# Attention scores: one copy of 1097 columns out of PSUM in place of two copies with a maximum each

## What is computed

```
attn = q @ k.T * SCALE                       # 1097 x 1097, head dimension 8
kth  = the 137th largest score of each row   # top_k = 1097 // 8
attn = softmax(where(attn >= kth, attn, -inf))
out  = attn @ v
```

## Time and profile before

| | |
|---|---|
| median of 3 runs | 11960.32 us (11940.51 to 11967.36) |
| the profiled execution | 11958.84 us, of which the span is 11957.0 us |
| busy over the span | DVE 9191.7 us (77%), PE 8171.2 us (68%), ACT 6947.3 us (58%), POOL 2151.1 us (18%) |
| the attention stage | 3009 to 10121 us from the span's start, 128 steps |
| copies out of PSUM (L1281) | 1280 from `a_psS`, 889.7 us busy; 1024 from `a_psT`, 703.0 us |

### The profile page before, as it was taken

One profiled execution on the slowest core, in us unless ns is written; L12 is line 12 of the kernel. 1 busy time (PEld: TensorE's weight loads), 2 busy tenths in 40 slices (PEclk: granted clock), 3 DMA queues, 4 the chain that ended last, 5 costly groups with the idle time before them and its releaser, 6 DMA issues. The chain is left out here.

```text
span 11957.0 us, 167569 instructions
## 1 busy us (share of the span) xinstructions
PE 8171.2 (68%) x45521; PEld 5352.0 (45%) x45521; DVE 9191.7 (77%) x26006; ACT 6947.3 (58%) x11527; POOL 2151.1 (18%) x1960
## 2 busy tenths in 40 slices
PE   5555477777486765667878687876667768343899
PEld 4555455555243433334444344443334434233787
DVE  8999644444898988999999899998889989644333
ACT  0000011221697976878999799997788979122222
POOL 2323211111000000000000000000000000277666
PEclk9999955555566655656666666665666656555555
DMA  3222100000000000000000000000000000243211
GB/s 91 73 68 72 33 19 20 20 19 21 14 16 16 17 12 14 13 16 17 17 17 18 14 15 18 18 18 14 13 14 17 18 12 16 43 96 79 55 54 40
DMA packets 669893, 352.03 MB, mean 29 GB/s; under 512 B 587281, under 2 KB 605680, under 8 KB 665056
## 3 DMA queue, kind: packets, MB, share of 16 engines
q1 hardware_dynamic: 607920, 242.84, 9.5%
q0 software_dynamic: 58624, 60.72, 2.0%
q10 hardware_dynamic: 2384, 37.11, 0.9%
HBM read 200.20 MB, written 147.72 MB: 29 GB/s over the span
## 5 line engine op out<-in xcount | busy, mean ns | idle before, releaser
L1049 PE MATMUL a_psT<-a_qt,a_kt 74*122 74x366 bf16 x3456 | 1554.8, 450 | 969.1 <-ACT a_pT L1130 632.0
L1138 ACT ACTIVATE a_junk<-a_s,a_aim 122x1097 bf16<-122x1097 f32 x1152 | 1378.9, 1208 | 721.3 <-DVE a_s L1281 721.3
L1214 DVE MAX8 a_near<-a_below 122x8 f32<-122x274 f32 (+1 forms) x4608 | 1699.2, 430 | 0.1
L1052 PEld LDWEIGHTS a_psT<-a_weigh,a_drops 122*122 122x122 bf16 x10368 | 1571.0, 190 | 192.0
L1207 DVE SCALAR_TENSOR_TENSOR a_below<-a_s,a_te,a_signs 122x1097 f32<-122x1097 f32 x1152 | 1546.4, 1352 | 129.2 <-remote 128.3
L1130 ACT ACTIVATE a_pT<-a_psT 122x732 f32<-122x732 f32 (+1 forms) x1920 | 1371.6, 715 | 455.4 <-PE a_psT L1052 447.9
L1052 PE MATMUL a_psT<-a_weigh,a_drops 122*122 122x122 bf16 x10368 | 1522.5, 273 | 0.0
L1138 ACT ACTIVATE a_signs<-a_s,a_te 122x1097 bf16<-122x1097 f32 x1152 | 1400.9, 1219 | 4.4 <-DVE a_te L1199 4.4
L1065 PE MATMUL a_psO<-a_pT,a_v 122*32 122x366 f32 x6912 | 1401.3, 698 | 0.0
L1138 ACT ACTIVATE a_junk<-a_s,a_te 122x1097 bf16<-122x1097 f32 x1152 | 1389.2, 1209 | 0.0
L1049 PEld LDWEIGHTS a_psT<-a_qt,a_kt 74*122 74x122 bf16 x3456 | 616.8, 178 | 1667.0 <-issue 1648.1
(11 more groups left out here) (356 smaller groups left out, 14795.9 us busy)
## 6 DMA issues: line engine op xcount, KB each, us to landing
xbuf<-r_blank ACTq DMA_DIRECT2D x16, 1990.6 KB
e_xg<-xbuf SPq DMA_DIRECT2D x56, 568.8 KB, 4.3
r_bc<-pr SPq DMA_DIRECT2D x16, 1372.0 KB, 7.4
a_k<-kT SPq DMA_DIRECT2D x384, 51.5 KB
a_q<-qT SPq DMA_DIRECT2D x384, 51.5 KB
a_kt<-kT SPq DMA_DIRECT2D x384, 51.5 KB
a_qt<-qT SPq DMA_DIRECT2D x384, 51.5 KB
r_xt<-in_x SPq DMA_DIRECT2D x16, 784.0 KB
```

The costliest lines, as they stand in the source:

```text
L1049: pe.matmul(out[:, x, 0:CW], kt[q][:, u * QP:(u + 1) * QP], qt[q][:, c * CW:(c + 1) * CW], start=True, stop=False)
L1052: mm = pe.matmul(out[:, x, t * QP:(t + 1) * QP], drops[:, c * CT + t, u * QP:(u + 1) * QP], weigh[:, :], start=False, stop=t == CT - 1)
L1138: act.activation(out[:, :], s_[:, t, :], ACT.Sign, bias=at[:, t:t + 1], scale=-1.0, accum_out=total[:, t:t + 1]).then_inc(counted[r], 1)
L1214: mx = dve.max(near[:, t, g, :], below[t % 3][:, EDGES[g]:EDGES[g + 1]])
```

## The change

A score tile now lies in consecutive columns for odd tiles too: `psT[0]` and `psT[1]` become two halves of one PSUM tensor `a_psB` of 4 banks, and an odd score tile takes its first 1097 columns. One DVE instruction copies the whole tile and keeps one maximum straight in `a_peak`; the `tensor_tensor` over the two maxima goes, and a bare semaphore increment stands in its place. PE raises `scored` once per tile, on the third matmul, and waits for `evacuated` once per tile, ahead of the first matmul; all counts of these two semaphores are halved accordingly. The fills keep their places in PSUM. No operation, transfer or tile is added.

```diff
-        peaks = sb("a_peaks", [QP, 2, QT])
-        psT = [ps(f"a_psT{i}", [QP, 2, 512]) for i in range(2)]
+        psB = ps("a_psB", [QP, 2048])
+        psT = [psB[:, 1024 * i:1024 * (i + 1)].rearrange("p (x n) -> p x n", x=2) for i in range(2)]
...
         def score_banks(t):
-            if t % 2:
-                return (psT[i][:, :, :].rearrange("p x n -> p (x n)") for i in range(2))
-            return psS[0:QP, 0:HALF], psS[0:QP, HALF:3 * HALF]
+            return (psB if t % 2 else psS)[0:QP, 0:MN]
...
-                wait(pe, evacuated, 2 * n - 1 if t == 0 else 2 * n - 3)
+                wait(pe, evacuated, n if t == 0 else n - 1)
                 apart(pe, k)
                 q_ = qs[o][:, t * QP:(t + 1) * QP]
-                low, high = score_banks(t)
-                pe.matmul(low[:, 0:HALF], q_, ks[o][:, 0:HALF], start=True, stop=True).then_inc(scored, 1)
+                out = score_banks(t)
+                pe.matmul(out[:, 0:HALF], q_, ks[o][:, 0:HALF], start=True, stop=True)
...
-                wait(pe, evacuated, 2 * n if t == 0 else 2 * n - 2)
...
-                pe.matmul(high[:, 0:HALF], q_, ks[o][:, HALF:2 * HALF], start=True, stop=True)
-                pe.matmul(high[:, HALF:MN - HALF], q_, ks[o][:, 2 * HALF:MN], start=True, stop=True).then_inc(scored, 1)
+                pe.matmul(out[:, HALF:2 * HALF], q_, ks[o][:, HALF:2 * HALF], start=True, stop=True)
+                pe.matmul(out[:, 2 * HALF:MN], q_, ks[o][:, 2 * HALF:MN], start=True, stop=True).then_inc(scored, 1)
...
-                banks = tuple(score_banks(t))
-                for i, (a, b) in enumerate(((0, HALF), (HALF, MN))):
-                    wait(dve, scored, 2 * (QT * (s + 1) + t) + i + 1)
-                    dve.tensor_scalar(sc[o][:, t, a:b], banks[i][:, 0:b - a], 1.0, None, ALU.mult, ALU.max,
-                                      accum_out=peaks[:, i, t:t + 1]).then_inc(evacuated, 1)
+                wait(dve, scored, QT * (s + 1) + t + 1)
+                dve.tensor_scalar(sc[o][:, t, :], score_banks(t), 1.0, None, ALU.mult, ALU.max,
+                                  accum_out=peak[:, t:t + 1]).then_inc(evacuated, 1)
...
                 if ahead:
-                    wait(dve, evacuated, 2 * QT * (s + 2))
-                    dve.tensor_tensor(peak[:, :], peaks[:, 0, :], peaks[:, 1, :], ALU.max).then_inc(peaked, 1)
+                    wait(dve, evacuated, QT * (s + 2))
+                    dve.sem_inc(peaked, 1)
```

More of the change, by code:

```diff
@@ L984, in step @@
                 if not isinstance(s, int) or s + 2 < HEADS:
-                    wait(sp, scored, 2 * QT * (s + 1))
+                    wait(sp, scored, QT * (s + 1))
                     operands(s + 2, qs[p], ks[p], s_in[p])
@@ L1079, in turn_back @@
                 wait(pe, o_out, CHUNKS * (s - 2))
-                wait(pe, evacuated, 2 * QT * done(s + 1))
+                wait(pe, evacuated, QT * done(s + 1))
                 wait(pe, flagged, 2 * done(s - 1))
@@ L1091, in step @@
                 if last:
-                    wait(pe, evacuated, 2 * QT * done(s + 1) - 2)
+                    wait(pe, evacuated, QT * done(s + 1) - 1)
                     for i in range(2):
@@ L1173, in step @@
                             wait(act, aimed, 5 * s + 6)
-                        wait(act, evacuated, 2 * (QT * (s + 1) + t + 1))
+                        wait(act, evacuated, QT * (s + 1) + t + 1)
                         if t >= 2:
```

## The result

The changed kernel takes 12015.45 us (median of 8 runs, 11978.02 to 12019.67), the kernel before on the same chip 11939.69 us (8 runs, 11919.42 to 11967.36): a ratio of 1.0053, 95% interval 1.0038 to 1.0068. The ratio is estimated from all runs of both kernels; the quotient of the two medians alone would be 1.0063. The changed kernel is slower, as forecast, and within the range given (11955 to 12030).

What follows compares the result with a forecast made beforehand. DVE's copies were taken to bound the attention stage, and PE's answer after the change. 91 steps gave +44.6 us, 13 gave -1.6, the others 0: 11958.84 + 43 + 1.5 = 12003 us, range 11955 to 12030.

Steps and rivals of the forecast that it cites:

- The body: Back-to-back copies of a step after tile 0's first; claimed paced by DVE before the change, with PE early.
- C: Way round for two tiles: copy with read 1.30, signal 0.15, PE's refill 0.89, signal 0.30; 2.64 us.
- the ordinary step: Step where DVE waited for tile 0; 11.50 us before, 11.99 after, +0.49 in 91 steps.
- The sum of the copies: Change over all 128 attention steps: 44.6 - 1.6 = +43 us.
- late steps: Up to 24 steps, one shown with ACT bounding the end; -0.08 to +0.10 us each, taken as 0.
- The ready steps: 13 steps with tile 0 ready and both its copies counted; 12.11 to 11.99 us, -0.12 each, -1.6 together.
- The last `tensor_tensor`: 0.17 us at each step's end, taken as hidden behind the sequencer: its removal gains 0, otherwise 22 us.
- Edits costed at nothing: ACT's later counts, PE's first fills of the next step and fewer PE register and semaphore instructions; 0 us.
- T0: Moment in each step when tile 0 is complete and its last copy can start; claimed not to move.
- ACT's cover: Time from tile 4 copied out to ACT beginning on it; about 1.9 us, claimed to hide later copies.
- the faster rival: PE answers in time in the body, needing its 2.4 GHz clock; 11915 to 11937 us, chance 0.07.
- the slowest rival: Wide copy pays for a second bank border; 0.40 us more per step, 12048 us, chance 0.05.

Runs made afterwards that it cites:

- e5: Kernel before, with an extra 256-column matmul on PE ahead of each tile but tile 0; 11955.11 us, ratio 0.9992.
- e4: Changed kernel, with an extra 256-column matmul on PE ahead of each tile but tile 0; 12074.34 us, ratio 1.0079.
- e2: Changed kernel, with a 9-column `tensor_tensor` carrying the increment in place of the bare one; 11992.95 us, ratio 1.0029 to the kernel before.
- e3: Changed kernel without DVE's wait for its last copy and the bare increment; PE waits for the copies' count instead; 11892.81 us, ratio 0.9957.
- e8: Kernel before, odd tiles in one PSUM tensor, last-copy wait and maximum moved behind the next step's first window; 11892.20 us, ratio 0.9945.
- e7: Changed kernel, tiles 0, 1, 4 and 5 copied and released in two parts, maximum over two columns; 11932.44 us, ratio 0.9983.
- e1: Kernel before, two copies per tile kept, but one whole-tile wait in either direction; 12078.29 us, ratio 1.0088.
- e10: Changed kernel, only tile 0 copied and released in two parts, maximum over two columns; 11961.1 us in one run.

## Why the prediction was right, and where its sum was off

- **What bounds the copies.** Right. The body was DVE's before (e5: PE's extra work cost nothing) and is PE's answer after (e4: it cost 0.21 us each round). C was forecast as 2.64 and is 2.64, link by link; the wide copy 1.22 with PE hearing of it after 1.30, as measured; the ordinary step 11.99, measured 11.97 or 11.98 in 96 of the 128 steps.
- **The sum of the copies.** +43 was forecast and +41.5 measured (36.5 + 5.8 - 0.8), but by errors that cancel. There were 32 late steps, not 24, and they lost 0.18 us each where 0 was taken; the 82 ordinary ones lost 0.445 on average and not 0.49, since 14 of them end at 11.78 to 11.88, about the 11.79 which the prediction gave for a step with PE's clock still high at tile 2, but reckoned with among the late steps alone. That the two sums lie so close is luck. The ready steps gained 0.14 where they were ordinary otherwise, against -0.12.
- **The last `tensor_tensor`.** This term was mis-sized: costed at nothing, with a gain of up to 22 us as its other bound. It cost 7.9 + 4.0 = 11.9 us, on the other side of both. The step that failed is to have looked at the operation that goes and not at what stands in its place: a bare increment with the wait. By the rule of the Trainium skill ("PSUM — Partial Sum Buffer", Engine vs sequencer instructions) that the sequencer waits only for dispatch, the small operation is hidden; e2 agrees, for with it the gap is 0.52 and without it not shorter. That rule says nothing of a semaphore wait on the engine's own result, and there e3 shows what it lacks: 0.61 with the wait and the increment, 0.00 without. That the sequencer stands still at such a wait fits e3 and e8, but no row shows the sequencer itself.
- **Edits costed at nothing.** T0 didn't move: from the end of the search (`a_bad`) to T0 the median is 5.30 us in both kernels. ACT's cover held: `move` waited for it 4 times in the stage, before 16 times. What is left of it at `move` is 0.91 us in the step shown, which e7 used up; the 1.9 us of the prediction, from the end of tile 4's copy to ACT's count of it, says how late the copies may come, and not how early `move` may.
- **The rivals.** The clock over the body is 0.50 as before (5093 to 5102), the 1.2 GHz level, and the faster rival fell. Its condition was right all the same: where the clock was still 1.00 the round took 2.45, which is DVE's copies alone, but that held in 34 of 384 rounds. The second bank border costs nothing: the pitch is 1.22 to 1.23, not 1.30, so the slowest rival fell too. The advice of the Trainium skill ("Perfetto Trace Analysis", Optimizing Scalar/DVE Operations) has both sides in it: larger operations where the engine is saturated, and breaking up where it isn't but causes bubbles on other engines. In the kernel before DVE's copies ran back to back, which is the first case, and the larger operation did save 97 us of DVE's busy time. e1 and e7 show that breaking up, where it lets PE start sooner, is worth more all the same.
- **Slips in the working.** 2.64 less the 0.06 of a faster hand-over is 2.58, not 2.57, so that the low bound of the sum is nearer +3 than 0; the slowest rival's 46 us more make 12049, not 12048; 14 steps were ready, not 13. Tile 1 was not whole before DVE asked for it: its third matmul starts at 5076.10 and takes 0.27, and DVE starts on its low part at 5076.14; it was whole before DVE's second copy at 5076.75. None of this moves the forecast.
- **The total.** The profiled executions differ by 58.7 us: 41.5 from the copies, 11.9 from the increment, 2.1 elsewhere in the stage, 2.7 ahead of it and 0.6 behind it.

## What to carry to other kernels

Merging two copies out of a double-buffered memory also merges two hand-overs. Add up the way round for the coarser unit (copy, signal, refill, signal) and compare it with the time the copying engine needs for all units in that round; only if the first is smaller does the saved fixed cost arrive (here 2.64 against 2.44, and it did not; where PE's clock was high, it did). And look for an engine that waits for its own last instruction: moving that wait behind the next long instruction, or letting the consumer wait instead, was worth more here than the change and its reversal.

## What had not been expected of the hardware

- Where DVE waited for a semaphore that its own last copy raises, the next window started 0.52 to 0.61 us behind that copy's accumulator read, and at once (0.00) without the wait (e3) or with it placed behind that window (e8). At the end of a pass of the hardware loop the difference was 1.5 us (3.85 to 2.34) and 1.1 us (3.71 to 2.66).
- A bare semaphore increment behind such a wait costs 0.09 us more than an operation of 9 columns that carries it (0.61 against 0.52).
- The stages behind the attention, the same code in all these kernels, took between 1800.8 and 1838.2 us in the profiled executions. Shown are the changed kernel and e4 behind the attention stage (columns as in the earlier trace rows); the granted clock of PE differs, and PE's busy time with it:

```profile
10179.00:12015.00 1836.00, 1192.34 (x7561) 995.88 (x7559) 828.27 (x1628) 455.36 (x830) 1111.49 (x1046) 0.53 0.25 60
```

```profile
10266.00:12066.00 1800.00, 1152.78 (x7563) 963.37 (x7561) 826.61 (x1628) 455.17 (x828) 1121.31 (x1046) 0.55 0.26 61
```

That is up to 37 us in code which no edit here touched, and in the profiled executions of e4 and e10 (1800.8 and 1801.0) it makes the totals lie lower than their stages would. What set it was not tested. The length of the attention stage, which differed by less than 1 us between the kernel before and e5, is the sharper measure of this change.
